# Causal attention scores on TensorE: 64-by-64 tiles in place of 64-by-128 for the masked half

## What is computed

```
x = x + tanh(g_xattn) * cross_attention(layernorm(x), ctx, ctx)      # no mask: "X half"
# "Y half": causal self-attention of the transformer block
q, k = rope(xn) @ Wq.T + bq, rope(xn) @ Wk.T + bk ; v = xn @ Wv.T + bv
scores = einsum('bqhd,bkhd->bhqk', q, k) * scale
scores = where(tril(ones(S, S)), scores, -inf)
ctx = einsum('bhqk,bkhd->bqhd', softmax(scores), v)
x1 = layernorm(xn + ctx @ Wo.T + bo)
# then the gate picks 2 of 8 experts, a second layernorm, "Z part"
x = x + tanh(g_ffn) * layernorm(x1 + moe(x1))
```

## Time and profile before

| what | value |
|---|---|
| median of 3 runs | 522.45 us |
| profiled execution, its time | 522.93 us |
| its span, first to last instruction | 521.1 us |
| TensorE matmul busy | 448.9 us (86%) |
| VectorE, GpSimd, ScalarE busy | 385.2, 323.7, 278.6 us |
| mean granted TensorE clock | 0.950 |

### The profile page before, as it was taken

One profiled execution on the slowest core, in us unless ns is written; L12 is line 12 of the kernel. 1 busy time (PEld: TensorE's weight loads), 2 busy tenths in 40 slices (PEclk: granted clock), 3 DMA queues, 4 the chain that ended last, 5 costly groups with the idle time before them and its releaser, 6 DMA issues.

```text
span 521.1 us, 15905 instructions
## 1 busy us (share of the span) xinstructions
PE 448.9 (86%) x5728; PEld 280.0 (54%) x5728; DVE 385.2 (74%) x1191; ACT 278.6 (53%) x693; POOL 323.7 (62%) x702
## 2 busy tenths in 40 slices
PE   0369788778888899999999999999789999999983
PEld 0134444444444456666666666666447666666652
DVE  6377878787786777767777777773269899999981
ACT  1126656666565665666656666666444554554530
POOL 1445654565468898887888878621044766667654
PEclk9999979888797999999999999999879999999995
DMA  4565775556343434344343443420000000000000
GB/s 108 127 170 132 183 173 128 125 141 152 94 108 95 103 91 98 86 106 110 96 98 85 105 115 93 98 70 10 3 0 11 12 20 23 10 22 11 23 20 20
DMA packets 88333, 42.70 MB, mean 82 GB/s; under 512 B 16312, under 2 KB 88128, under 8 KB 88256
## 3 DMA queue, kind: packets, MB, share of 16 engines
q1 hardware_dynamic: 79040, 39.59, 30.8%
q10 hardware_dynamic: 9216, 2.10, 2.0%
HBM read 5.75 MB, written 2.10 MB: 15 GB/s over the span
## 4 chain that ended last, share of the span: by engine, by line
PE 32%; DVE 20%; POOL 17%; issue 6%; ACT 2%; POOLq 0%; ACTq 0%; DVEq 0%
PE u_bank L421 6%; DVE z_acc L922 5%; PE s_bank L374 4%; PE s_bank L364 4%; POOL xn_all L238 4%; PE u_bank L773 2%; POOL rstd L233 2%; PE u_bank L434 2%; PE s_bank L752 2%; DVE nm L599 2%; POOL rc L256 2%; PE st_bank L752 2%; PE t_bank L346 2%; POOL z_rstd_ L650 2%; DVE stats L555 1%
## 5 line engine op out<-in xcount | busy, mean ns | idle before, releaser
L599 DVE TENSOR_REDUCE nm<-s_bank 128x4 f32<-128x512 f32 x256 | 173.1, 684 | 73.5 <-PE s_bank L374 71.7
L499 ACT ACTIVATE pt<-st_bank 128x512 f32<-128x512 f32 x256 | 150.0, 598 | 102.6 <-PE st_bank L374 60.4
L374 PE MATMUL s_bank<-qk 64*128 64x128 bf16 x1024 | 105.7, 231 | 11.3 <-DVE nm L599 7.7
L421 PE MATMUL u_bank<-pt,vaug 128*32 128x128 f32 x2048 | 113.8, 296 | 0.0
L374 PE MATMUL st_bank<-qk 64*128 64x128 bf16 x1024 | 106.4, 227 | 0.0
L374 PEld LDWEIGHTS s_bank<-qk 64*128 64x128 bf16 x1024 | 70.7, 99 | 39.2 <-issue 27.7
L374 PEld LDWEIGHTS st_bank<-qk 64*128 64x128 bf16 x1024 | 71.4, 98 | 0.4
L421 PEld LDWEIGHTS u_bank<-pt,vaug 128*32 128x32 f32 x2048 | 41.4, 111 | 29.0 <-issue 4.1
L364 PE MATMUL s_bank<-mqk,esel 64*128 64x256 bf16 x256 | 49.7, 274 | 0.4 <-ACT pt L499 0.4
L364 PE MATMUL st_bank<-mkq,esel 64*128 64x256 bf16 x256 | 49.7, 274 | 0.0
L280 POOL TENSOR_TENSOR part<-r,part 128x512 bf16<-128x512 f32 x32 | 37.1, 1159 | 2.7
(11 more groups left out here) (118 smaller groups left out, 904.3 us busy)
## 6 DMA issues: line engine op xcount, KB each, us to landing
qk<-part SPq DMA_DIRECT2D x224, 128.0 KB, 2.6
x_all<-x SPq DMA_DIRECT2D x16, 128.0 KB, 2.6
c_all<-ctx_in SPq DMA_DIRECT2D x16, 128.0 KB, 2.8
qk<-qrow SPq DMA_DIRECT2D x32, 64.0 KB, 2.1
qk<-mts ACTq DMA_DIRECT2D x64, 32.0 KB, 2.6
out<-z_o SPq DMA_DIRECT2D x16, 128.0 KB, 1.8
ewt<-exp_t SPq DMA_DIRECT2D x1, 512.0 KB
qk<-krow SPq DMA_DIRECT2D x4, 64.0 KB, 2.0
```

The lines of the kernel that those rows point to most:

```text
L374: return pe.matmul(bank[:, j * P:(j + 1) * P], k if keys_first else q, q if keys_first else k, start=not masked, stop=True, skip_group_che ...
L421: ins = pe.matmul(u_bank[b][32 * j:32 * j + 32, r * P:(r + 1) * P], v, pt[m % 4][:, j, :], start=half == 0, stop=half == 1, skip_group_che ...
L499: act.activation(pt[m % 4][:, :, :].rearrange("k j q -> k (j q)"), st_bank[m % 2][:, :], ACT.Exp).then_inc(ex, 1)
L599: dve.tensor_reduce(nm[q % 2][:, first:first + HEADS], s_bank[n % 2][:, :].rearrange("q (j k) -> q j k", j=HEADS), AX_X, ALU.max, negate=T ...
```

## The change

The masked tiles use 64 columns of the array in place of 128. A triangle multiplies by a 64-by-64 piece of the identity `idb` and writes only the 64 partitions in which its block lies; the table `esel` and its four DMAs go (`LATER` from 28 to 24). Each product of a masked tile becomes two matmuls, one for each half of the output partitions, each with 64 stationary columns and the same 128 moving columns. Products of unmasked tiles keep 128 stationary columns.

```diff
-EARLY, LATER = 4, 28
+EARLY, LATER = 4, 24
...
-        esel = sb("esel", [P, 2, P], BF16)
...
-                if s == 5:
-                    for half in range(2):
-                        for block in range(2):
-                            sp.dma_start(esel[64 * half:64 * half + 64, block, :],
-                                         identb[64 * block:64 * block + 64, :]).then_inc(c_late, 16)
...
             def triangle(bank, mask, block, half):
                 rows = slice(64 * half, 64 * half + 64)
-                to = bank[:, :].rearrange("p (j k) -> p j k", j=HEADS)[:, :, 64 * block:64 * block + 64]
-                pe.matmul(to, esel[rows, block, :], mask[rows, rows].unsqueeze(1).broadcast_to([64, HEADS, 64]),
-                          start=block == 0, stop=False, skip_group_check=True)
+                outs = slice(64 * block, 64 * block + 64)
+                to = bank[outs, :].rearrange("p (j k) -> p j k", j=HEADS)[:, :, outs]
+                pe.matmul(to, idb[rows, rows], mask[rows, rows].unsqueeze(1).broadcast_to([64, HEADS, 64]),
+                          start=True, stop=False, skip_group_check=True)
...
-                masked = in_y(u)
-                return pe.matmul(bank[:, j * P:(j + 1) * P], k if keys_first else q, q if keys_first else k,
-                                 start=not masked, stop=True, skip_group_check=masked)
+                fixed, moving = (k, q) if keys_first else (q, k)
+                to = bank[:, j * P:(j + 1) * P]
+                if in_y(u):
+                    for block in range(2):
+                        outs = slice(64 * block, 64 * block + 64)
+                        ins = pe.matmul(to[outs, :], fixed[:, outs], moving, start=False, stop=True, skip_group_check=True)
+                    return ins
+                return pe.matmul(to, fixed, moving, start=True, stop=True)
```

## The result

The changed kernel takes 541.05 us (median of 4 runs, 538.42 to 543.42), the kernel before 521.39 us in the same session: a ratio of 1.0379, with a 95% interval of 1.031 to 1.0448. It is slower by 3.8%, where 0.6% was forecast and the range ended at 535. The direction was right and the size was not.

The account below looks back on a forecast made before the run. TensorE was taken as nearly never idle from slot 141, steady units as a loop through VectorE, GpSimd and TensorE. 522.93 - 7.5 + 10.9 = 526.3, median 0.5 lower: 525.8 us, 0.6% slower; range 513.5 to 535.

Parts of the forecast that it names:

- The one on the clock: Slots 128 to 140, as sparse as the first half: a tenth of their time at half clock, 1 to 2 us more.
- the sum: Whole kernel: 7.5 us saved in masked slots, 10.9 lost in slots 128 to 140; 526.3 us profiled, 525.8 median.
- The mixed slots' changes of shape: Slots 128 to 140, `n` 64x64 and `m` 64x128 alternating: seven changes, 1.44 us up to `av`, 0.89 more each, +10.9 us.
- the rival without a drain: Slots 128 to 140: no drain between halves of the rows, so they save 0.09 us too; 514.3 us, chance 0.25.
- Triangles and products where both are masked: Steady units and tail: four triangles together, products still 0.055 us a head; 0.09 us saved, slot of 0.81 us.
- the rival of slow instructions: All masked slots: instructions come too slowly, 0.12 us a slot lost; 545 us; chance 0.15 with weights, 530 to 545.
- The gain of the steady units and the tail: 11 steady units, four slots each in the loop, save 4.0 us; 39 tail slots save 3.5; together -7.5 us.
- First half and last part: The X half and the Z part should stay within a microsecond; if they move, it is the clock.

Follow-up runs that it names:

- `every_fourth`: Changed kernel, but of slots 128 to 140 only 128, 132, 136 and 140 alternate 64x64 and 64x128, the other nine are all 64x64; 517.61 us.
- `grouped`: Changed kernel, but in slots 128 to 140 all products of `n` come first, then all of `m`, one shape change inside the scores; 519.0 us.
- `uniform`: Changed kernel, but in slots 128 to 140 the unmasked products of `m` are also made 64 columns wide; 516.92 us, ratio 0.9919.
- `uniform_sp`: `uniform`, but the DMA of the maxima's rows is issued from SyncE's queue in place of ScalarE's; 514.77 us, ratio 0.987.
- `grouped_two`: Changed kernel, but in slots 128 to 140 two heads of `n` and two of `m` are made in turn, three shape changes; 526.35 us.
- `filled`: Changed kernel with its seven shape changes kept, but each unmasked product of `m` in slots 128 to 140 is made four times; 557.55 us.

## Why the prediction was wrong, point by point

**Which step failed.** The one on the clock: "A tenth of their time at half clock is 1 to 2 us more." It was named as a rival, and the sum put the clock at nothing. Its price was about right, its share was not: of the 43.67 us of the mixed slots all but the first 1.5 were at half clock, a mean of 0.52. At full clock the sum says 18.18 + 13 x 0.89 - 0.7 = 29.1 us for them; slot 128 of the changed kernel and the four slots with seven changes in `every_fourth`, 1.44 us each from triangle to `av`, bear the 0.89 out. So 14.6 us are the clock's. I had judged these slots from TensorE's busy share and mean clock in the first half. The busy share says little: it is 43.67 of 43.67 us in the mixed slots, since recorded durations overlap the gaps.

The whole difference adds up for the profiled execution: 526.3 forecast, 14.6 for the clock, 3.3 that the masked slots gained less, 0.6 behind the mixed slots, less 1.3 in the first half and the last part, is 543.5; it took 543.42. Why the clock falls in these slots stays open; the runs show that it did not fall in them with one change a slot (`grouped`), with seven in every fourth (`every_fourth`) or with none (`uniform`).

**The mixed slots' changes of shape: right.** Forecast 1.44 us from triangle to `av`, measured 1.44. Changes between the two halves of the rows cost what the others do, 0.11 us with the weights; the rival without a drain is out. The Trainium skill (TensorEngine Tiling (Array Packing), Key Properties) says that changing the tiling mode drains TensorE, and the gaps at these changes agree.

**Triangles and products where both are masked: right.** Slot 0.81 to 0.82 us, forecast 0.81; products at 0.055 us a head with 16 matmuls; the rival of slow instructions is out. The distance of about 25 ns between starts, which the Trainium skill (TensorE: Matmul & The Clock Gate, "Wait — 56ns, not 53.3ns?") gives for small matmuls, doesn't hold between different tiles in this trace: four start within 0.01 to 0.02 us, 16 in 0.18.

**The gain of the steady units and the tail: little more than half of it came.** "In the steady units only the four slots inside the loop count ... 4.0 us saved" gave 2.1, "39 x 0.09 = 3.5" gave 2.1. ScalarE's exponential, behind a DMA issue of 0.54 us, became the last to come. I had called the loop bound by TensorE, VectorE and GpSimd and hadn't asked what ScalarE would be late with at 0.81 us a slot. That is the second step that failed, worth 3.3 us. `uniform_sp` takes that issue away and gives 0.35 us a unit and 3.3 us in the tail.

**The rest.** First half and last part moved by 1.1 and 0.2 us. That is noise: slot 128 starts at 184.0 in `grouped_two` and at 187.5 in `filled`, whose first halves are the same.

## What to carry to other kernels

Before changing the tile shape of some matmuls, list what stands between them in program order: a change of shape cost about 0.11 us at full clock wherever it came here, also between halves of the rows that otherwise run side by side, and a boundary between two phases of a pipeline may interleave both shapes for as long as its lag. Order by shape, or give the neighbours the same shape even where it gains them nothing, which cost nothing here. A stretch with many changes of shape may also be at half the clock, as it was here; look at the granted clock there, not at the busy share. And when a slot gets 10% shorter, walk down every other engine's queue for what was just in time, DMA issues included.

## What the runs showed of the hardware

- Four 64x64 tiles run together: four triangles of 256 columns in the time of one, and twice as many matmuls and weight loads at the same 0.055 us a head.
- A change between 64x64 and 64x128 tiles on different halves of the rows costs 0.11 us at full clock, with the weights that are then no longer hidden (0.78 us from triangle to `av` with one change, 1.00 with three, 1.44 with seven).
- A DMA issue on ScalarE's queue holds ScalarE for 0.54 us, and what stands behind it comes late.
- The clock was at half through nearly all of 13 slots with seven changes each (mean 0.52), at half after nine slots with three changes (mean of the stretch 0.76), and full with one change a slot or with seven in every fourth slot. With products of `m` repeated between the seven changes it was 0.57. With `av` repeated in six of the slots it was full but for two falls, and the kernel with more work took 537.4 against 541.05 us. What decides it stays open.
